# Graph attention: first-edge logits by 0/1 products on TensorE instead of 49 scatters, own edges joined at the nodes, 42 staged groups

## The reference

```python
def _gat_conv(x, src, dst, ea, W, a_src, a_dst, We, a_edge, bias):
    h = x @ W
    al_s = h @ a_src
    al_d = h @ a_dst
    al_e = ea_full @ We @ a_edge
    alpha = jax.nn.leaky_relu(al_s[s] + al_d[d] + al_e, 0.2)
    amax = jax.ops.segment_max(alpha, d, num_segments=n)
    ex = jnp.exp(alpha - amax[d])
    denom = jax.ops.segment_sum(ex, d, num_segments=n)
    coef = ex / (denom[d] + 1e-16)
    out = jax.ops.segment_sum(h[s] * coef[:, None], d, num_segments=n)
    return out + bias
```

## Time and the profile before

| what | value |
| --- | --- |
| median of 3 runs | 8075.14 us |
| lowest and highest run | 8069.89, 8077.05 us |
| the profiled execution | 8068.22 us |
| its span (first to last instruction) | 8065.2 us |
| busy: PE, DVE, ACT, POOL | 5008.3, 5106.6, 1997.2, 4900.1 us |
| mean granted TensorE clock | 0.731 of full speed |

### The profile page before, as it was taken

How to read it: one execution, slowest core, us unless ns; L and a number is a source line. 1 busy time by engine, 2 the same in 40 slices (tenths; PEclk the granted TensorE clock), 3 DMA queues, 4 the chain that set the end, 5 groups by cost and what they waited for, 6 DMA issues and landing times.

```text
span 8065.2 us, 102051 instructions
## 1 busy us (share of the span) xinstructions
PE 5008.3 (62%) x25982; PEld 3322.5 (41%) x25982; DVE 5106.6 (63%) x17152; ACT 1997.2 (25%) x3703; POOL 4900.1 (61%) x5045
## 2 busy tenths in 40 slices
PE   5555556666557777699999772542763533755533
PEld 3444443333334444444444442532533533424532
DVE  7787567777659999700001496853797844787744
ACT  6666654343316666600000000000100000000000
POOL 6777747777647777500000477777677776777774
PEclk8777777777668888899999756765656756556755
DMA  6555557677515555588888423321233321234311
GB/s 178 167 155 154 155 151 205 196 205 199 152 42 201 215 214 214 200 307 291 284 288 291 153 92 115 117 62 37 71 117 108 117 53 43 77 113 123 92 53 32
DMA packets 728901, 1216.86 MB, mean 151 GB/s; under 512 B 109340, under 2 KB 547085, under 8 KB 714832
## 3 DMA queue, kind: packets, MB, share of 16 engines
q1 hardware_dynamic: 552716, 847.76, 31.3%
q0 software_dynamic: 161120, 311.32, 14.9%
q10 hardware_dynamic: 14688, 53.48, 1.7%
HBM read 865.31 MB, written 346.85 MB: 150 GB/s over the span
## 4 chain that ended last, share of the span: by engine, by line
POOL 55%; issue 19%; PE 17%; DVE 7%; DMA 1%; ACT 1%; SPq 0%; DVEq 0%; POOLq 0%; ACTq 0%
POOL RO L1022 26%; POOL RO L981 26%; PE PS L1549 13%; POOL nd L1004 2%; DVE RO L2396 1%; PE PS L1662 1%; POOL at_first L997 1%; PE PS L1502 1%; POOL acc L1039 1%; DVE H L2408 1%; DMA RO<-table,src_t 0%; DVE acc L1985 0%; PE PS L1374 0%; PE PS L1347 0%; DVE shared L2115 0%
## 5 line engine op out<-in xcount | busy, mean ns | idle before, releaser
L1022 POOL DMA_INDIRECT RO<-table,src_t x2346 | 2244.9, 957 | 1995.3 <-DMA table<-H 1238.3
L981 POOL DMA_INDIRECT RO<-table,src_t x2346 | 2312.9, 986 | 958.4 <-issue 759.6
L1985 DVE TENSOR_TENSOR acc<-acc,PS 128x128 f32 x3910 | 1091.7, 279 | 1064.2 <-PE PS L1589 761.4
L1589 PE MATMUL PS<-RO 128*128 128x128 f32 x3060 | 689.5, 416 | 1172.5 <-DMA RO<-table,src_t 1151.4
L1589 PEld LDWEIGHTS PS<-RO 128*128 128x128 f32 x3060 | 636.9, 317 | 1217.0 <-DMA RO<-table,src_t 1196.0
L2214 DVE TENSOR_SCALAR RO<-PS,loc_t,shared 128x128 f32<-128x128 f32 x2346 | 940.0, 402 | 0.4
L1502 PE MATMUL PS<-RO 128*128 128x128 f32 x3128 | 604.6, 373 | 405.6 <-DMA RO<-table,src_t 391.2
L1502 PEld LDWEIGHTS PS<-RO 128*128 128x128 f32 x3128 | 572.1, 281 | 494.6 <-DMA RO<-table,src_t 468.8
L1287 ACT ACTIVATE small<-small 128x49 f32<-128x49 f32 x3 | 0.7, 246 | 2019.5 <-DVE small L2460 2019.5
L1662 PEld LDWEIGHTS PS<-als_bf,RO 128*128 128x128 bf16 x7056 | 308.5, 119 | 427.0 <-DVE RO L2396 269.7
L1147 ACT ACTIVATE H<-PS 128x392 f32<-128x392 f32 x784 | 394.8, 504 | 339.9 <-PE PS L1482 333.8
(11 more groups left out here) (403 smaller groups left out, 8832.4 us busy)
## 6 DMA issues: line engine op xcount, KB each, us to landing
GT<-adjacency SPq DMA_DIRECT2D x126, 1792.0 KB, 7.2
adjacency<-H SPq DMA_DIRECT2D x98, 1568.0 KB
RO<-adjacency SPq DMA_DIRECT2D x42, 1792.0 KB, 7.2
RO<-table,src_t POOLq DMA_INDIRECT x4692, 3.2
staged<-RO ACTq DMA_DIRECT2D x102, 512.0 KB
H<-staged SPq DMA_DIRECT2D x102, 512.0 KB, 3.7
soft_rows<-shared SPq DMA_DIRECT2D x196, 256.0 KB
H<-soft_rows SPq DMA_DIRECT2D x98, 512.0 KB, 3.9
```

The costliest lines, as they stand in the source:

```text
L981: pool.indirect_dma_start(rows[:, h * HT + j, :], None, table[k % 2], at(src_t[:, t:t + 1]))\
L1022: pool.indirect_dma_start(rows[:, g % 2 * HT + j, :], None, table[k % 2], at(src_t[:, t:t + 1]))\
L1589: last = mm(PS[:, o:o + D], block[:, j * D:(j + 1) * D], onehot[:, h * HT + j, :], start=True, stop=True)
L1985: tt(at, at, window_at(k, c, j), ALU.add).then_inc(added[h], 1 if j < n - 1 else HT - n + 1)
```

## The change

The scatters to DRAM and the load of that array go. The positions of the nodes' first edges are split into a lane (0 to 127) and a place in the lane (0 to 783). For each of the 49 node tiles DVE makes two matrices: which lane (128x128, 0 or 1) and al_d at the place (128x784); TensorE multiplies them in fp32 and adds all 49 products up in two PSUM banks, which then hold al_d at the first edges, in the scan layout. This is done for one node tile in each iteration of the loop of logits. The own edges' logit is not spread over the edges any more: the edges take their own maximum, and the nodes rescale with exp(m - max) when both are joined in `self_weights`. `SG` goes from 34 to 42.

```diff
-SG = 34
+SG = 42
-SCATTER_AFTER = 8
...
+                def first_values(t):
+
+                    pe.wait_ge(first_hot, t + 1 + l * NT)
+                    for to, part in first_parts:
+                        opening = isinstance(t, int) and t == 0
+                        last = mm(to, first_lane, first_row[:, part], start=opening, stop=True,
+                                  skip_group_check=not opening)
+                    last.then_inc(first_added, 1)
+
                 pe.wait_ge(first_in, l + 1)
                 for h in range(2):
                     spread(0, h)
+                first_values(0)
                 with pe.Fori(0, ITERS - 1) as i:
                     for h in range(2):
                         candidates(i, h)
                         spread(i + 1, h)
+                    first_values(i + 1)
...
-                carries(5)
+                carries(4)
...
-                step(copy(nd3[:, :, 0], ald_n))
-                step(copy(nd3[:, :, 1], self_n), first_in)
+                step(copy(place_n, firstpos[:]), first_in)
+                step(ts(lane_n, place_n, 0.5, 1.0 / ET, ALU.add, ALU.mult))
+                step(ts(lane_n, lane_n, -0.5, MAGIC, ALU.add, ALU.add))
+                step(ts(lane_n, lane_n, -MAGIC, None, ALU.add))
+                step(stt(place_n, lane_n, -float(ET), place_n, ALU.mult, ALU.add))
+                for q in range(ET // TB):
+                    step(ts(place_iota[:, q * TB:(q + 1) * TB], iota_row[:, 0:TB], float(q * TB), None, ALU.add))
...
+                def first_hots(t):
+                    v.wait_ge(first_added, t + l * NT)
+                    hold(v)
+                    lane = ts(first_lane, iota_row[:], lane_n[:, ds(t, 1)], None, ALU.is_equal)
+                    if isinstance(t, int):
+                        step(lane)
+                    ts(first_row, place_iota, place_n[:, ds(t, 1)], ald_n[:, ds(t, 1)], ALU.is_equal, ALU.mult)\
+                        .then_inc(first_hot, 1)
...
                 make_lo(0, 0)
+                first_hots(0)
                 with v.Fori(0, ITERS - 1) as i:
                     make_lo(i, 1)
                     pick(i, 0)
                     make_lo(i + 1, 0)
                     pick(i, 1)
+                    first_hots(i + 1)
                 make_lo(ITERS - 1, 1)
+                v.wait_ge(first_added, (l + 1) * NT)
+                for of, part in first_parts:
+                    step(copy(Gs[1][:, part], of))
...
-                v.wait_ge(first_ld, 16 * (l + 1))
                 add, spread = (ALU.add, ALU.max), (ALU.mult, ALU.add)
-                step(scan(*linked_scan(Gs[3], same_s[:], at_f[:, :, 0], spread, col(ALLSAME), 0.0)))
-                step(scan(*linked_scan(Gs[4], same_s[:], at_f[:, :, 1], spread, col(ALLSAME), 0.0)))
+                step(scan(*linked_scan(Gs[3], same_s[:], Gs[1], spread, col(ALLSAME), 0.0)))
...
-                step(tt(at_l[:, :, 1], Gs[7], Gs[4], ALU.max))
-                step(tt(Gs[5], Gs[0], at_l[:, :, 1], ALU.subtract), exp_in)
+                step(tt(Gs[5], Gs[0], Gs[7], ALU.subtract), exp_in)
+                step(copy(at_l[:, :, 1], Gs[7]))
                 zero_acc(k)
```

More of the change, by code:

```diff
@@ L422, in build @@
         back = H[:, ACCW - 2 * GROUP_WORDS:ACCW]
-        at_f = G[:, ET:3 * ET].rearrange("p (j c) -> p j c", c=2)
+        lane_n, place_n = nd[:, 0:NT], nd[:, NT:2 * NT]
+        first_row = acc[:, 3 * ET:4 * ET]
+        place_iota = acc[:, 4 * ET:5 * ET]
+        first_lane = acc[:, 5 * ET:5 * ET + P]
+        first_parts = [(PS[:, 3072:3072 + 4 * TB], slice(0, 4 * TB)), (PS[:, 3584:3584 + 3 * TB], slice(4 * TB, ET))]
         at_l = H[:, 0:2 * ET].rearrange("p (j c) -> p j c", c=2)
@@ L431, in build @@
         als_n, ald_n, self_n, amax_n, exs_n, rden_n = (small[:, i * NT:(i + 1) * NT] for i in range(6))
+        edge_and_self, edge_share = small[:, 3 * NT:5 * NT], amax_n
         mean_var = small[:, 6 * NT:8 * NT].rearrange("p (t c) -> p t c", c=2)
@@ L600, in build @@
         first_in = sem("first_in")
-        first_sc = sem("first_sc")
-        first_ld = sem("first_ld")
+        first_hot = sem("first_hot")
+        first_added = sem("first_added")
         last_in = sem("last_in")
@@ L920, in _ @@
                     neighbour_edges()
-                    sp.wait_ge(zeros_ready, 1)
-                    sp.dma_start(at_first.rearrange("(p j) c -> p (j c)", p=P), acc[:, 0:2 * ET]).then_inc(zeros_stored, 16)
                     other_inputs()
@@ L991, in in_step_with_logits @@
                         pool.wait_ge(al_rows[1], i - LOGITS_BEHIND + l * ITERS)
[L993 to L998, removed]
                 def gather_lasts(l):
@@ L1286, in _ @@
                     s.wait_ge(exp_in, 2 * (k - 4))
-                    nc.scalar.activation(exs_n, exs_n, ACT.Exp).then_inc(exp_out, 1)
+                    nc.scalar.activation(edge_and_self, edge_and_self, ACT.Exp).then_inc(exp_out, 1)
                     copy_ranks(k)
@@ L2459, in self_weights @@
                 step(tt(amax_n, nd3[:, :, 1], self_n, ALU.max))
-                step(tt(exs_n, self_n, amax_n, ALU.subtract), exp_in)
+                step(tt(exs_n, self_n, amax_n, ALU.subtract))
+                step(tt(edge_share, nd3[:, :, 1], amax_n, ALU.subtract), exp_in)
                 v.wait_ge(exp_out, 2 * (l + 1))
-                step(tt(rden_n, nd3[:, :, 0], exs_n, ALU.add))
+                step(tt(rden_n, nd3[:, :, 0], edge_share, ALU.mult))
+                step(tt(rden_n, rden_n, exs_n, ALU.add))
                 step(ts(rden_n, rden_n, 1e-16, None, ALU.add))
@@ L2465, in self_weights @@
                 step(tt(own_weight_ps, exs_n, rden_n, ALU.mult))
+                step(tt(rden_n, rden_n, edge_share, ALU.mult))
                 step(tt(rden_n, rden_n, count[:], ALU.mult))
@@ L2525, in _ @@
                     first_ranks()
-                    step(memset(acc[:], 0.0), zeros_ready)
+                    step(memset(acc[:], 0.0))
                 if k in DENSE:
```

8 lines of the change are left out of this document (removed).

## The result

The changed kernel takes **8245.42 us** (median of 4 runs, 8240.18 to 8252.08) against 8072.8 us for the kernel before in the same comparison: the ratio is 1.0216, with a 95% interval of 1.0202 to 1.0231. It is slower by some 173 us. The forecast was 8217 us (8130 to 8325).

A forecast was written before the change was run, and what follows sets the result against it. POOL's issuing was taken to bound the kernel before; after, POOL waits for the logits loop. Layer ends move 33.9, 53.9 and 53.9 us, together 142: 8068 + 142 = 8210, median 6.9 above, so 8217 us (8130 to 8325).

The forecast's parts named there:

- POOL bounds, with some 50 us of room in the others: Attention layers: POOL never waits for another engine; a longer logits loop costs nothing for some 50 us, then every microsecond.
- What is removed: POOL's 49 scatters per layer, 63 us; if nothing makes POOL wait, a layer is 62.8 us shorter.
- rival (2): Nothing waits: products hide beside DVE, or DVE is ready before staging; needs iterations under 6.7 us; 7887 us, chance 0.02.
- The circle: Logits loop: products, candidates, pick, make_lo, pick, lane and place matrices follow in turn; 9.08 us an iteration against 5.36.
- The clock: TensorE in the logits loop: products run at the low clock, 1.2 GHz, taking 2.62 us in place of 1.31.
- rival (1): TensorE's clock rises and stays in the logits loop: iteration 7.24 us, 7948 us in all; chance 0.10, 0.12 with mixtures.
- The sum: Exponential's argument 169.9 us later, group 44 starts 23.9 us after it; POOL stands 97, 117, 117 us; together 142 us slower.
- (3): Rival: longer loop iteration, 9.9 us, by narrow-rate products and a slower place matrix; 8335 us; an edge of the 0.83 case.
- (4): Rival: shorter loop iteration, 8.7 us, by quicker candidates and no first weights; 8159 us; an edge of the 0.83 case.
- The sign's point, 8.1 us: Logits loop: the iteration length at which the change's total effect is zero, neither faster nor slower.

The follow-up runs named there:

- e8: Changed kernel without the lane and place matrices and the products in the loop, the scan reading zeros; dst logits at first edges left out: 7880.24 us.
- e12: Changed kernel with the products late (middle of the next body) plus eight dummy fp32 products of 64 columns ending each iteration on TensorE: 7887.23 us.
- e3: Kernel before the change with 42 staged groups in place of 34 and nothing else: 8057.5 us, ratio 0.9991.
- e4: Changed kernel with each iteration's products moved on TensorE from the body's end to the middle of the next body, nothing left out: 7884.28 us.
- e7: Changed kernel with ten dummy fp32 products of 128 columns ahead of the 0/1 products in each iteration: 8014.09 us, ratio 0.9925.
- e1: Changed kernel with the products cut to one column per part from the second node tile on, matrices and waits kept: 7977.32 us, ratio 0.989.
- e11: Changed kernel with twenty dummy fp32 products of 64 columns ahead of the 0/1 products in each iteration: 8241.62 us, ratio 1.0228.
- e10: Changed kernel with constant 1.0 in place of the al_d column as the place matrix's second scalar: 8244.35 us.

## Why the prediction was right

- *POOL bounds, with some 50 us of room in the others.* Right: e8 and e12 show a time set by POOL's issues, and e3 that later staging gives it nothing. The room can be read from e4: in the second and third layer its argument starts 61.4 us later behind the first gather than before, and POOL waits 6.36 and 7.56 us, 0.30 of each for its own issuing. That is a room of some 54 to 55 us, against 53.2 by the prediction's terms.
- *What is removed: 62.8 us a layer if nothing waits.* Right: e8 is 8075.6 - 7880.2 = 195.4 us below the kernel before of its session, 65.1 a layer; rival (2)'s 7887 us is within 7 us of e8 and e4.
- *The circle.* Right as a mechanism: e4 opens it by moving the products alone, and gets 361 us. Its size was the term most off: 9.40 us in place of 9.08. The means over the 144 rounds, by the starts in the timelines of PE and DVE: products and first weights 2.78 (2.72 put), candidates to first pick 1.36 (1.43), the picks 1.64 and 1.48 with `make_lo` 1.20 (1.49, 1.49, 1.19), the lane matrix 0.20 (0.14), the place matrix and the way to TensorE 0.74 (0.62). These are +0.06, -0.07, +0.15, -0.01, +0.01, +0.06 and +0.12, together the 0.32: most of it is the first pick behind the wait and the two matrices, which I had taken from rows of other instructions. From the candidates to the first pick it was 1.03 to 1.46, shorter where the clock had risen for them.
- *The clock.* Right: in each of the 144 rounds 2.77 or 2.78 us lie between the products' start and the candidates', where e7 has 1.42 at the high clock; the mean over the loop was 0.60. The clock rose behind the products in some rounds, so TensorE's wait for the place matrix is 3.1 us and not some 2. e7 shows that the clock decides the sign, as rival (1) had it, and that the case comes when TensorE's gap is filled. The price of rival (1) was too low: 7.24 us against 7.71, and 7948 us against 8001 to 8014. That the throttled clock is the default and activity releases it (the Trainium skill, "TensorE: Matmul & The Clock Gate", "What's actually happening") agrees with e7's 0.95. With the fp32 work that the change itself adds, the loops stayed at 0.59 to 0.60.
- *The sum.* In the first layer the argument's operation starts 543.4 us behind the first gather (5073.3 - 4529.87), before 357.7 (4881.66 and a first gather at 4523.95): 185.7 us later, against the 169.9 of the forecast. The difference is about 48 x 0.33. From the argument to group 44 it is 22.3 us (23.9 put). POOL stood 118.3, 120.2 and 120.2 us (97, 117, 117 put). In the first layer that is 21 us more, by the longer iteration and by an arrival at group 44 that came 7.5 us sooner behind the first gather than put. In the others it would be the same 21, but the 18 us by which the loop holds POOL back came off it. The prediction left that wait out, although its own 9.08 us is longer than seven issues; as it falls ahead of the stall it moved no time. The profiled execution came out 183.9 us longer, 142 put: 46 from the iteration (144 x 0.32), 6 from a later start of the first attention layer (4529.87 against 4523.95), whose cause I did not look for, and some 9 less by the shorter way to group 44 and the rate of 1.271.
- *The rivals.* (2) needs iterations below 6.7 us: e4 with 6.82 and 14.2 us of stall puts that point well. (3) was refuted on its place matrix (0.68, not 1.14 us); (4) was too low. The sign's point, 8.1 us, was not run, but lies on the line through e7 (7.74 us, 8001 to 8014) and the changed kernel (9.40, 8245), which crosses 8073 at 8.2.

## What to carry to other kernels

Hidden work in an in-order queue is hidden only if nothing that the other engine waits for stands behind it: ask of each added instruction what it holds up, then how long it is. Here the same products cost 361 us more at the body's end than in its middle, where they and their matrices cost at most some 15. And where one engine paces a layer, find its first wait on the others: work is free up to that moment and costs one for one beyond it, so a buffer count such as `SG` and the length of a loop have to be judged together.

## What the runs showed of the hardware

- **More TensorE work, less time.** Ten useless fp32 products an iteration raised the granted clock from 0.60 to 0.95 and made the changed kernel 231 us faster (e7).
- **Fp32 matmuls of 64 columns are bound by something other than columns:** 0.128 us each for 64 columns at a clock of 0.91, 0.125 for 128 columns at 0.95, and in e1 four of one column held the next work up for 0.88 us at a low clock. By the wide rate of the earlier trace rows (0.429 us for 512 columns at 1.00) columns alone would make it 0.107 us for 128 and 0.054 for 64, an estimate: those of 128 are near it, those of 64 take over twice as long.
- **Opening a sum drops the others of its bank.** In e11 and e12 the dummies open a sum in 64 columns that nothing else uses, in the bank in which the products' first part is added up. In both, the norm of the output's difference from the reference is 0.4073 of the reference's norm. The reference computed without al_d for the edges of the nodes of tiles 0 to 47 whose first edges stand in places 0 to 447, which is the first part of all products but the last, differs by 0.4073 too. So each opening made the next product overwrite the sum. The Trainium skill says so ("PSUM — Partial Sum Buffer", "PSUM: the matmul accumulator"): two groups open in one bank cannot both begin with the flag that clears. The runs agree.
- **A second scalar operand from SBUF** costs DVE some 0.06 us on 128x784 in fp32 (0.68 against 0.62, e10).
